# Windowed attention: values weighted before they are projected, and softmax weights turned in 32x32 blocks by VectorE

## The reference

```python
w = WINDOW                                   # 32; HEADS 16, DIM_HEAD 64
bk2, bv2 = (look(bk), look(bv))              # window before and own window: 64 keys
sim = jnp.einsum('bhwie,bhwje->bhwij', bq, bk2) * QK_SCALE
sim = jnp.where(mask, -jnp.finfo(sim.dtype).max, sim)
attn = jax.nn.softmax(sim, -1)
out = jnp.einsum('bhwij,bhwje->bhwie', attn, bv2)
...
for i in range(DEPTH):                       # 6
    x = attn_layer(shift_tokens(x), Wqkv[i], q_scale[i], k_scale[i], Wo[i]) + x
    x = ffn_layer(shift_tokens(x), ln_g[i], ln_b[i], W1[i], b1[i], W2[i], b2[i]) + x
```

## Time and profile before

| | |
|---|---|
| median of 3 runs | 1619.39 us (1618.85 to 1620.7) |
| the profiled execution | 1619.38 us, its span 1617.6 us |
| busy: PE, DVE, ACT, POOL | 1544.3, 1234.8, 1232.5, 1222.1 us |
| granted TensorE clock over the span | 0.987 |

### The profile page before, as it was taken

The page is one execution under the profiler, slowest core; times in us unless marked ns, Lnnn a source line. Parts: engine busy times, 40 slices in busy tenths (PEclk is TensorE's granted clock), DMA queues, the critical chain, the costliest instruction groups (busy, mean ns, idle before and its releaser), DMA issues.

```text
span 1617.6 us, 69676 instructions
## 1 busy us (share of the span) xinstructions
PE 1544.3 (95%) x30224; PEld 907.8 (56%) x30224; DVE 1234.8 (76%) x1693; ACT 1232.5 (76%) x2368; POOL 1222.1 (76%) x1051
## 2 busy tenths in 40 slices
PE   7879999999999999999999999999999999999995
PEld 6745556555555555555556555555565565555553
DVE  5488878778778778777877778778778788787873
ACT  4347787787787787887887887887887887887871
POOL 6169888777787778778777787787787787787861
PEclk9989999999999999999999999999999999999998
DMA  5000000100000100000100000100000000000000
GB/s 193 28 2 27 10 7 5 61 7 6 22 6 7 35 29 10 18 7 9 36 28 10 9 16 10 33 31 9 9 16 9 7 5 9 7 18 9 7 12 27
DMA packets 24545, 32.60 MB, mean 20 GB/s; under 512 B 2372, under 2 KB 21424, under 8 KB 23344
## 3 DMA queue, kind: packets, MB, share of 16 engines
q1 hardware_dynamic: 24240, 28.15, 5.4%
HBM read 20.80 MB, written 1.05 MB: 14 GB/s over the span
## 4 chain that ended last, share of the span: by engine, by line
PE 75%; ACT 7%; issue 5%; DVE 3%; POOL 1%; DMA 0%; ACTq 0%; SPq 0%; POOLq 0%; DVEq 0%
PE ring L274 20%; PE psq L254 18%; PE ring L262 9%; PE ring L308 8%; PE pss L292 7%; PE ring L325 4%; PE ring L318 4%; PE pss L283 2%; DVE qb L927 2%; ACT L1126 2%; ACT sq L1096 1%; ACT uT L1126 1%; ACT pr L1100 1%; ACT kT L1107 1%; PE ring L649 1%
## 5 line engine op out<-in xcount | busy, mean ns | idle before, releaser
L254 PE MATMUL psq<-wqk,x0S 128*128 128x512 f32 x768 | 379.4, 617 | 4.0 <-issue 3.1
L274 PE MATMUL ring<-mh,x0S 128*32 128x512 f32 x3072 | 369.6, 598 | 7.4 <-ACT uT L1126 7.4
L1305 POOL TENSOR_TENSOR qa<-qa,qb 128x1024 f32<-128x1024 f32 x96 | 228.9, 2384 | 63.0 <-DVE qb L848 62.9
L1361 POOL TENSOR_TENSOR pr<-pr,rden 128x1024 f32<-128x1024 f32 x96 | 183.9, 1915 | 88.3 <-DVE rden L824 88.0
L1357 POOL TENSOR_TENSOR qa<-qa,qb 128x1024 f32<-128x1024 f32 x96 | 226.7, 2361 | 0.4 <-DVE qb L927 0.3
L254 PEld LDWEIGHTS psq<-wqk,x0S 128*128 128x128 f32 x768 | 135.8, 192 | 130.0 <-issue 120.8
L308 PEld LDWEIGHTS ring<-u,pT 128*32 128x32 f32 x6144 | 172.9, 111 | 61.4 <-issue 61.4
L904 DVE TENSOR_TENSOR qa<-psq,tab 128x1024 f32<-128x1024 f32 x96 | 117.5, 1224 | 105.5 <-PE psq L254 105.5
L308 PE MATMUL ring<-u,pT 128*32 128x128 f32 x6144 | 187.0, 274 | 3.2 <-ACT pT L1228 3.2
L1323 POOL TENSOR_TENSOR qa<-qa,rn 128x1024 f32<-128x1024 f32 x96 | 182.7, 1903 | 7.5
L274 PEld LDWEIGHTS ring<-mh,x0S 128*32 128x32 f32 x3072 | 80.0, 109 | 190.5 <-issue 172.6
(11 more groups left out here) (174 smaller groups left out, 2819.8 us busy)
## 6 DMA issues: line engine op xcount, KB each, us to landing
wqk<-in_wqk SPq DMA_DIRECT2D x6, 1024.0 KB, 4.9
mvT<-in_mvT SPq DMA_DIRECT2D x6, 512.0 KB, 5.6
wo<-in_wo SPq DMA_DIRECT2D x6, 512.0 KB, 8.7
xf<-x SPq DMA_DIRECT2D x24, 128.0 KB
xf<-x SPq DMA_DIRECT2D x24, 127.0 KB
rope<-in_rope SPq DMA_DIRECT2D x1, 2048.0 KB, 10.0
w<-in_w SPq DMA_DIRECT2D x6, 341.0 KB, 3.8
xmid<-in_x SPq DMA_DIRECT2D x4, 256.0 KB, 4.0
```

The lines of the kernel that those rows point to most:

```text
L254: return mm(psq[:, 512 * (n % 2):512 * (n % 2) + 512], x0S[:, tile * P:tile * P + P], wqk[:, l % 2, 512 * n:512 * n + 512], start=True, st ...
L274: last = mm(bank[WIN * g:WIN * g + WIN, :], x0S[:, tile * P + WIN * w:tile * P + WIN * w + WIN], mh[:, l % 2, g, :, :].rearrange("p j n -> ...
L1305: g_.tensor_tensor(qa[:, t % 2, 0:1024], qa[:, t % 2, 0:1024], qb[:, 0:1024], ALU.add).then_inc(sum_q, 1)
L1361: g_.tensor_tensor(p4[t % 2], p4[t % 2], rden[:, :].unsqueeze(1).unsqueeze(3).broadcast_to([P, 2, HEADS, WIN]), ALU.mult).then_inc(p_ready, 1)
```

## The change

- `values`, `turn_p` and their six ScalarE copies are gone. VectorE turns `pr` into `pT` with one instruction, `transpose`, which transposes each 32x32 block by itself. That puts each window's keys on the 32 rows of that window.
- `weighted` (banks V0 to V3, one for each window) multiplies 32 raw tokens (`xb`: the window before, `xa`: the own window; stationary, 32 rows by 128 columns) by `pT` (32 rows, 512 columns: 16 heads by 32 queries). Two such products add up in each of the four banks, on the four groups of 32 rows. ScalarE copies the four banks into `zT` with a stride.
- `mix` (Y) now multiplies `zT` of each head (128x128) by M_h (128x128) and sums over the 16 heads: sixteen whole-array products.
- `xa` and `xb` are copies of the tokens on other partitions (shifted by one token in the second half; `xb` shifted by a window as well). SP makes them with seven SBUF-to-SBUF DMAs for each unit or group (`spread`), 25 times.
- The order of all engines within a step is written anew, and the lags with it. Semaphores `l_bst` and `l_rs` are split in two.

```diff
-            def values(bank, t, w):
-                tile, l = t % TILES, t // TILES
-                for g in range(4):
-                    last = mm(bank[WIN * g:WIN * g + WIN, :], x0S[:, tile * P + WIN * w:tile * P + WIN * w + WIN],
-                              mh[:, l % 2, g, :, :].rearrange("p j n -> p (j n)"), start=True, stop=True)
-                return last
...
-            def turn_p(banks, t):
-                halves_turned(banks, lambda blk: pr[:, t % 2, blk * P:blk * P + P])
+            def weighted(banks, t):
+                for e in range(2):
+                    for w in range(NWIN):
+                        rows = slice(WIN * w, WIN * w + WIN)
+                        last = mm(ring[banks[w][0]][:, :], (xb, xa)[e][rows, t % TILES, :, :].rearrange("p a n -> p (a n)"),
+                                  pT[rows, e, :], start=(e == 0), stop=(e == 1))
+                        if e == 1:
+                            last.then_inc(filled[banks[w][0]], 1)
             def mix(bank, t):
-                for b in range(4):
-                    for half in range(2):
-                        for w in range(NWIN):
-                            slot, v_w = (t % 2, w - 1 + half) if w + half > 0 else ((t + 1) % 2, NWIN - 1)
-                            last = mm(bank[WIN * w:WIN * w + WIN, 0:P],
-                                      pT[:, half, b * P + WIN * w:b * P + WIN * w + WIN],
-                                      u4[:, slot, v_w, b * P:b * P + P],
-                                      start=(b == 0 and half == 0), stop=(b == 3 and half == 1))
+                for h in range(HEADS):
+                    last = mm(bank[:, 0:P], zT[:, t % 2, h, :, :].rearrange("p w q -> p (w q)"),
+                              mh[:, t // TILES % 2, h % 4, h // 4, :], start=(h == 0), stop=(h == HEADS - 1))
                 return last
...
+                t = s - 3                      # TensorE
+                if 0 <= t < STEPS:
+                    banks = [take("V%d" % w, t) for w in range(NWIN)]
+                    pe.wait_ge(xab_ready, 16 * NSPREAD * copies_of(t))
+                    pe.wait_ge(pt_ready, t + 1)
+                    for bank, n in banks:
+                        wait(pe, freed[bank], n)
+                    weighted(banks, t)
...
+                    bank, n = take("Y", t)
+                    for w in range(NWIN):
+                        zbank, m = place["V%d" % w, t]
+                        pe.wait_ge(freed[zbank], m + 1)
+                    wait(pe, freed[bank], n)
+                    mix(ring[bank], t).then_inc(filled[bank], 1)
...
+                t = s - 3                      # VectorE
+                if 0 <= t < STEPS:
+                    dve.wait_ge(p_ready, t + 1)
+                    for w in range(NWIN if t > 0 else 0):
+                        bank, n = place["V%d" % w, t - 1]
+                        dve.wait_ge(filled[bank], n + 1)
+                    v.transpose(pT[:, :, :].rearrange("p e n -> p (e n)"), pr[:, t % 2, :]).then_inc(pt_ready, 1)
...
+                    bank, n = place["V3", t]   # ScalarE; V0, V1, V2 likewise
+                    act.wait_ge(filled[bank], n + 1)
+                    nc.scalar.copy(zT[:, t % 2, :, 3, :], ring[bank][:, :].rearrange("p (h q) -> p h q", q=WIN)).then_inc(freed[bank], 1)
...
+            def spread(k, t0, size):           # SyncE
+                wait(sp, xab_ready, 16 * NSPREAD * k)
+                here, last = slice(t0, t0 + size), min(t0 + size, TILES - 1)
+                front, behind = slice(t0, last), slice(t0 + 1, last + 1)
+                for dst, src in ((xa[:, here, 0, :], x0T[:, here, 0:HD]),
+                                 (xa[1:P, here, 1, :], x0T[0:P - 1, here, HD:P]),
+                                 (xa[0:1, behind, 1, :], x0T[P - 1:P, front, HD:P]),
+                                 (xb[WIN:P, here, 0, :], x0T[0:P - WIN, here, 0:HD]),
+                                 (xb[0:WIN, behind, 0, :], x0T[P - WIN:P, front, 0:HD]),
+                                 (xb[WIN + 1:P, here, 1, :], x0T[0:P - WIN - 1, here, HD:P]),
+                                 (xb[0:WIN + 1, behind, 1, :], x0T[P - WIN - 1:P, front, HD:P])):
+                    sp.dma_start(dst, src).then_inc(xab_ready, 16)
```

More of the change, by code:

```diff
@@ L585, in _ @@
-                t = s - 6
-                if 0 <= t < STEPS:
-                    bank, n = take("U0", t)
-                    if t % TILES == 0:
-                        for j in range(QUAD):
-                            mbank, m = place["H%d" % j, t // TILES]
-                            pe.wait_ge(freed[mbank], m + 1)
-                    wait(pe, freed[bank], n)
-                    values(ring[bank], t, 0).then_inc(filled[bank], 1)
-                if chunk_at(s - 4, 2) >= 0:
-                    chain_w(chunk_at(s - 4, 2))
@@ L871, in _ @@
+                    v.scalar_tensor_tensor(uT[0:rows, 2, :], ring[bank][0:rows, :], par[0:rows, i // GROUPS, 4:5],
+                                           uT[0:rows, 2, :], ALU.add, ALU.mult).then_inc(freed[bank], 1)
                 i = group_at(s, 13)
@@ L933, in _ @@
                 if 0 <= t < STEPS:
[L934 to L940 removed]
+                    dve.wait_ge(exp_done, t + 1)
```

823 lines of the change are left out of this document (394 added, 429 removed).

## The result

The changed kernel takes 1630.41 us (median of 15 runs, 1620.34 to 1637.93), the kernel before, timed beside it, 1620.24 (15 runs, 1617.46 to 1625.92): ratio **1.0062, 95% interval 1.0052 to 1.0073**. The forecast was 1609 and faster; 1630 lies inside the range of 1572 to 1640, but only because the range had taken in rivals that did not come about.

A forecast was written before the change was run, and what follows sets the result against it. It took TensorE's own work to set the time: 1619.4 us, less 38 for shorter blocks, less 12 for waits that go, plus 40 for new stalls, gives about 1609 us; range 1572 to 1640.

The forecast's parts named there:

- TensorE's work, per tile: TensorE's blocks: new `mix` 3.84 and `weighted` 1.85 replace 6.09 us, net -0.40 us a tile, -38 us in all.
- rival 3: `weighted`'s four row groups overlap only in part: 2.25 us gives 1637 (chance 0.13), 3.64 us about 1745 (0.07).
- ScalarE's work and the new wait: X and `mix` wait for ScalarE's copies in one step of four, k's projection slightly in every eighth: +40 us.
- -12 and +40: Waits of three touched TensorE blocks that go, -12 us; new TensorE stalls, mostly for ScalarE's copies, +40 us.
- VectorE's work: VectorE's added transpose, 1.2 us a tile, is hidden before q's projection ends, with 0.4 us of cover: priced at nothing.
- The copies of tokens: The 25 times seven DMAs, 7.4 us for each group, end well before `weighted` needs them: priced at nothing.
- The start and the last group keep their structure: nothing.: Beginning and end of the run: the change was claimed to add no time there, priced at nothing.
- Rival 1: `mix` never waits for ScalarE's copies, so the whole gain of 50 us is kept: 1569 us, chance 0.20.
- rival 2: VectorE takes over: its transpose or jitter delays q's rotary products; 1638 us at 1.8 us, 1693 at 2.38; chance 0.18.

## Why the prediction was wrong

- **"TensorE's work, per tile"** held. `weighted` 1.93 (1.85) and `mix` 3.67 (3.84): -0.49 us a tile instead of -0.40. One row group at a time would be 7.28 us by the pace of `project`, so four overlap 7.28/1.93 = 3.8 times. The 3.07 of the Trainium skill ("TensorE: Matmul & The Clock Gate", Measured speedup vs the span model) would have given an estimated 2.4 us; this trace, with 32-bit floats and sixteen records, does not agree, and rival 3 is out.
- **"ScalarE's work and the new wait"** held for the step that it walks: in tiles 12 to 84, X and `mix` wait 12.8 + 10.2 = 23.0 us, 0.32 a tile against 0.42. It counts 24 steps with X; there are 20. That its total of 40 us was measured as 37.8 is luck: 13.2 of `mix`'s 23.4 us lie outside tiles 12 to 84, in steps where nothing of a group stands between, which I had not walked.
- In the middle, then, the waits grew by 21.1 us, where -12 and +40 for 96 tiles make +21 for 72, and the gain is 14.5 us instead of 7.5 because the blocks are shorter still than forecast.
- **"VectorE's work"** at nothing: the turn took 1.24 us, and TensorE never waits for it in the changed kernel. The cover for more of it is thicker than 0.4. Whether the turn is free in the steps without group work is open.
- **"The copies of tokens"** at nothing held but for one wait of `weighted` for xb, 1.7 us at 1184.4. Their packets are far cheaper than the 0.058 us taken from the queue's mean: (8.7% of 1630.4 less 5.4% of 1617.6) x 16/50471 = 0.017 us each.
- **The step that failed: "The start and the last group keep their structure: nothing."** Tiles 0 to 12 take 9.0 us more, tiles 84 to 95 13.7, and the tail 5.1. For the tail every added length counts in full: the chain from scaling to addition is 10.5 instead of 4.1 us, and the earlier trace rows with the prediction's own prices give 1.2 + 1.85 + 4 x 0.58 + 3.84 = 9.2 against 3.7. For the start, the walk without X would have given the waits of `mix`, but not the whole: with V3's copy moved to two other places tiles 0 to 12 still take 187.7 and 188.9 us. What lengthens the start stays open.
- **A term that was missing:** waits of TensorE for its instructions, and half the clock behind long waits. The waits grew by 11 us, from 12.4 to 23.5; 8.9 of them, against 0.3, stand in tiles 84 to 95. Together with `mix`'s waits of 1.88 and 3.29 us and about 7 us of lower clock they make the +13.7 there. With half a block more ahead of everything, only 1.9 us of them fall there, and these tiles take 165.5 us, 1.5 more than before; so most of that loss seems to be a matter of where the blocks' borders fall. In tiles 12 to 84 the waits for nothing took back 2.1 us (12.1 against 10.0), not more. The earlier trace rows has a trace of the term, the 4.4 us of "issue" ahead of `turn_p`, which the prediction passed over. That the position in the block makes the waits is shown by the two runs with a set position; what the half clock alone costs was not separated from the wait ahead of it.
- Rival 1 is out, since X and `mix` wait; rival 2 is out as well, since the turn is 1.24 us and TensorE does not wait for it. But with less work on TensorE the loops over the other engines bind at 14.2 to 14.8 us a step, so only 71 us came of 177 us less of TensorE.

Of the start, tiles 0 to 4 are 5.7 us longer, and this was only read: the windows 113 to 128 and 128 to 143 us show a granted clock of 0.72 and 0.94 against 1.00 and 0.89 before. No run tested it. The order of the engines within a step and the lags were changed together with the blocks, and no run took the one without the other; that the order, and not the blocks, costs the time at the start is a rival that stands.

## What to carry to other kernels

A saving that is counted in the steady step has to be counted again in the steps with nothing to cover, the first and the last: there the chain can be what counts, and a longer chain with less work is then a loss, as in the tail here. Before trusting work taken from the busiest engine, leave half of one block out and look at how far the time falls: the next bound shows at once (here 71 of 177 us). Where a few hundred small instructions go by in under 2 us, look at the waits for nothing in the middle of them, and at which tiles they stand in, before blaming transfers.

## What the runs showed of the hardware

- TensorE's instructions come in blocks of 16384 bytes, 256 instructions. A block used up in about 1.6 us can make it wait, mostly on instruction 196 or 197: up to 3.2 us in the changed kernel. With the scores set on that position 58 of 96 tiles waited in them, 28 of these for 1 us or more; with the scores set to position 60 only the last did.
- An extra instruction on TensorE's queue that only checks a semaphore already reached cost 39 to 40 ns on average, behind a projection of 1.8 us. In tiles 12 to 84, steps with 7 of them took 15.8 us instead of 15.6, steps with 39 took 17.6 instead of 15.6.
- In the changed kernel's layers, up to the last scores, all three waits of TensorE over 2 us, and three of the eight from 1.78 to 1.91, had about 3.4 us at the lower clock behind them: `mix` 5.44 instead of 3.8 us, k's projection 2.9 instead of 1.9.
- Four groups of 32 rows with 512 columns in 32-bit floats overlap 3.8 times. VectorE's turn of 128x1024 numbers of 32 bits in 32x32 blocks takes 1.24 us, about the same as its other instructions of that size (1.21 to 1.22).
